# A pipelined decoder layer on one core: other mixtures, norm shifts on VectorE, low-rank halves, four product buffers, and another order

## The chip, the cores and the metric

The kernel runs on one core of a Trainium2 chip. The metric is the device time of one execution in microseconds (us). Everything is float32.

## The reference

The input `x` has 32 sequences of 256 tokens with 256 channels; `ctx` has the same shape. Three blocks are added to `x` in turn, each on a layer norm of it:

```python
# 1: RWKV layer
h  = layer_norm(n1, ln1_w, ln1_b); hh = h of the token before (0 for the first)
xk, xv, xr = h * tm + hh * (1 - tm)            # three mixtures with their own tm
k, v, sr = xk @ Wk.T, xv @ Wv.T, sigmoid(xr @ Wr.T)
y  = n1 + (sr * wkv(decay, first, k, v)) @ Wo.T     # a scan over the tokens
h  = layer_norm(y, ln2_w, ln2_b); xk, xr = two more mixtures
y  = y + sigmoid(xr @ Wrec.T) * (square(relu(xk @ Wkey.T)) @ Wval.T)
x  = x + y
# 2: attention of the 16 heads of one token among each other (16 values each)
x  = x + softmax(mask(q @ k.T / 4)) @ v       # q = norm(x), k = v = ctx, per token
# 3: low-rank feed-forward, rank 64
x  = x + (gelu((norm(x) @ U1) @ V1 + b1) @ U2) @ V2 + b2
```

## The kernel before

Two sequences, 512 tokens, make a group; there are NG = 16 groups. A group passes through five stages, and in step i of the program the engines work on group i-1 (here called A: mixtures, k, v, r, scan), i-2 (B: output projection, second norm, first key projections), i-3 (C: keys, values, third norm, attention scores) and i-4 (D: attention sums, fourth norm, low-rank block). `drive` lays the steps out: some unrolled ahead, a loop over pairs of steps, and some unrolled behind.

The program is written per engine. Each engine has a function `step` that lists its pieces in a fixed order with the semaphore waits between them; an engine works strictly in that order. TensorE (PE) does projections and transposes into eight PSUM banks of 512 columns; ScalarE (ACT) does activations; VectorE (DVE) does scans, residuals, statistics and sums of products; GpSimd (POOL) forms the products of the attention (`score_products`, `value_products`) and some sums and products of the scan; SyncE (SP) issues loads and stores.

- Norms: DVE takes statistics (`stats_of`, line 1154) and `mean_of` (1161). ACT forms ln of the variance and the negated mean (`variance_ln`, 440 and 441), rstd (`rstd_of`, 445), the shift -mean * rstd as four one-column activations (`shift_of`, 473), and `normalise` (480). For norm 1 there is also `back` (`scale_back`, 465), by which the normalised rows are scaled back.
- Mixtures: `now_part` (504, 506) writes the first token's column and then the present token's share from PSUM, `add_before` (1196) adds the share of the token before on DVE.
- Low-rank block: `project_u1` (904) writes the same 64 rows twice into one bank of 512 columns; `project_v1` (913) uses upper and lower half of the array in turn for even and odd output tiles; `project_u2` (920) sums even tiles in rows 0 to 63 and odd ones in rows 64 to 127; `project_v2` (932) multiplies with a doubled V2. `open_with_b2` (926) writes the bias. Each float32 matmul runs as two passes, each with its own weight load.
- Table loads: `use_table` (427) switches ACT between a set with exp and ln and one with tanh and gelu, four times per step.
- POOL works through D's scores 1 to 3 and values, and C's score block 0 at the end of its step; the products go through three buffers `prod`, so that a block waits for the sums of an earlier one.
- The norm chain ends in q (`normalise_3`), for which POOL's `score_products` (329) waits. `add_bb` on POOL forms the denominator, ACT's `ln_den` and `inverse_den` its reciprocal, and `divide_num` on POOL the numerator that `project_o` needs. `values_by_dim` (575) copies ctx.

## Time and profile before

| what | value |
|---|---|
| three runs, us | 1201.68, 1202.70, 1202.82; median 1202.7 |
| span of the profiled execution, us | 1199.4 |
| PE, DVE, ACT, POOL busy, us | 1020.8, 952.5, 940.2, 901.1 |
| PE weight loads busy, us | 586.0 |
| mean granted TensorE clock | 0.947 |

The profiled execution has no time of its own beside the span; the runs lie 1.8 to 3.4 us outside the span. Busy time is the time in which an engine executes at least one instruction. Pieces that follow each other directly overlap a little, so the mean time of an instruction times its count is more than the busy time.

### The profile page before, as it was taken

The page shows a single profiled execution, that of the slowest core. Times are in us where ns is not written, and L with a number is a line of the kernel's source. Part 1 is how long each engine was busy: PE and PEld are TensorE (multiplying, and loading weights), DVE is VectorE, ACT ScalarE, POOL GpSimd, SP SyncE. Part 2 cuts the span into 40 slices and gives each one's busy share as a digit, 9 for nine tenths or more (in the row PEclk, how much of TensorE's full clock was granted, in tenths as well). Part 3 has the DMA queues.
Part 4 walks back from the last instruction along what each step waited for, and adds up shares of the span by engine and source line. Part 5 has one row for each costly group of instructions (what it writes and reads, how often), then busy time and mean ns, then how long its engine had stood idle before and what let it go on. Part 6 is the DMA issues. An engine that isn't in the chain of part 4 may idle for free.

```text
span 1199.4 us, 14602 instructions
## 1 busy us (share of the span) xinstructions
PE 1020.8 (85%) x3584; PEld 586.0 (49%) x3584; DVE 952.5 (79%) x2092; ACT 940.2 (78%) x2007; POOL 901.1 (75%) x862
## 2 busy tenths in 40 slices
PE   2569698989899898989899898989898998969506
PEld 1237264654647363655646373645546473727202
DVE  3654889898989899798979898898979888757470
ACT  3778779888888979888888889888888888584504
POOL 0220997969696988969696978969696969978780
PEclk9889799999999999999999999999999999989767
DMA  5010020201111020201111110202011010201000
GB/s 176 18 23 31 1 53 1 71 0 54 18 54 19 9 62 1 72 0 53 18 53 18 33 38 1 72 0 62 9 53 36 17 37 0 54 1 36 1 17 18
DMA packets 38983, 38.54 MB, mean 32 GB/s; under 512 B 2932, under 2 KB 38648, under 8 KB 38904
## 3 DMA queue, kind: packets, MB, share of 16 engines
q1 hardware_dynamic: 30456, 29.38, 7.4%
q0 software_dynamic: 8448, 8.39, 4.6%
q14 instruction: 64, 0.52, 0.1%
q8 instruction: 15, 0.25, 0.1%
HBM read 29.38 MB, written 8.39 MB: 31 GB/s over the span
## 4 chain that ended last, share of the span: by engine, by line
PE 46%; ACT 25%; DVE 13%; issue 7%; POOL 6%; SPq 1%; DMA 0%; ACTq 0%; POOLq 0%; DVEq 0%
PE bank L832 18%; PE bank L889 12%; PE bank L920 5%; ACT n L480 4%; PE bank L839 4%; DVE bank L1345 4%; POOL prod L329 3%; ACT shift L473 3%; ACT q L480 3%; PE bank L913 3%; PE bank L932 2%; POOL prod L350 2%; DVE stat L1154 2%; ACT hidden L598 1%; ACT rr L546 1%
## 5 line engine op out<-in xcount | busy, mean ns | idle before, releaser
L329 POOL TENSOR_TENSOR prod<-q,kv_ctx 128x256 f32<-128x256 f32 (+5 forms) x448 | 360.1, 853 | 140.6 <-ACT q L480 140.6
L350 POOL TENSOR_TENSOR prod<-prob,v_dh 128x256 f32<-128x256 f32 (+3 forms) x256 | 383.9, 1606 | 0.0
L832 PE MATMUL bank<-xk,w_key 128*128 128x512 f32 x512 | 233.4, 605 | 11.3 <-DVE xk L1196 11.3
L889 PE MATMUL bank<-w_val,hidden 128*128 128x256 f32 x1024 | 225.9, 379 | 0.0
L1345 DVE TENSOR_REDUCE bank<-prod 128x64 f32<-128x256 f32 (+3 forms) x256 | 192.0, 819 | 34.8 <-POOL prod L350 25.4
L889 PEld LDWEIGHTS bank<-w_val,hidden 128*128 128x128 f32 x1024 | 193.5, 190 | 31.7 <-issue 6.7
L1318 DVE TENSOR_REDUCE score<-prod 128x16 f32<-128x256 f32 (+5 forms) x448 | 177.1, 466 | 19.5 <-POOL prod L329 19.4
L832 PEld LDWEIGHTS bank<-xk,w_key 128*128 128x128 f32 x512 | 97.7, 193 | 127.7 <-issue 111.0
L846 PE MATMUL bank<-ident,n 128*128 128x128 f32 x384 | 66.2, 302 | 103.4 <-ACT n L480 101.0
L565 ACT ACTIVATE hidden<-bank 128x512 f32<-128x512 f32 x128 | 74.1, 593 | 82.8 <-PE bank L832 82.7
L846 PEld LDWEIGHTS bank<-ident,n 128*128 128x128 f32 x384 | 49.3, 155 | 159.6 <-issue 153.7
L366 POOL TENSOR_TENSOR num<-num,rr 128x512 f32<-128x512 f32 x32 | 45.0, 1406 | 62.6 <-ACT rr L555 62.6
L427 ACT ACT_TABLE_LOAD x70 | 89.8, 1283 | 2.1 <-PEq L1494 0.9
L832 PE MATMUL bank<-xr,w_r 128*128 128x512 f32 x128 | 74.4, 711 | 16.9 <-DVE bb L1254 16.9
L598 ACT ACTIVATE hidden<-bank,vec 128x512 f32<-128x512 f32 x128 | 79.5, 710 | 6.3 <-PE bank L913 6.1
L832 PE MATMUL bank<-xk,w_k 128*128 128x512 f32 x128 | 64.4, 630 | 21.1 <-DVE xk L1196 21.1
L375 POOL TENSOR_TENSOR num<-num,aa 128x512 f32<-128x512 f32 x32 | 38.3, 1197 | 54.1 <-DVE num L1245 54.1
L1196 DVE SCALAR_TENSOR_TENSOR xk<-bank,prev_w,xk 128x510 f32<-128x510 f32 x64 | 47.1, 744 | 37.7 <-ACT xk L506 19.1
L569 ACT ACTIVATE hidden<-hidden 128x512 f32<-128x512 f32 x128 | 76.4, 627 | 0.0
L1364 DVE TENSOR_TENSOR y_out<-bank,x 128x512 f32<-128x512 f32 x32 | 22.0, 687 | 68.0 <-PE bank L932 67.9
L913 PE MATMUL bank<-pT,w_v 64*128 64x512 f32 x256 | 69.2, 640 | 6.4 <-ACT pT L594 6.3
L1154 DVE BATCH_NORM_STATS2 stat<-x 128x6 f32<-128x256 f32 x192 | 71.2, 413 | 1.7
(95 smaller groups left out, 1909.9 us busy)
## 6 DMA issues: line engine op xcount, KB each, us to landing
x_in<-in_x SPq DMA_DIRECT2D x16, 512.0 KB, 3.5
x<-in_x POOLq DMA_DIRECT2D x16, 512.0 KB, 5.7
kv_ctx<-in_ctx SPq DMA_DIRECT2D x16, 512.0 KB, 4.5
out<-y_out SPq DMA_DIRECT2D x16, 512.0 KB, 3.2
w_key<-in_wkey SPq DMA_DIRECT2D x1, 1024.0 KB
w_val<-in_wval SPq DMA_DIRECT2D x1, 1024.0 KB
w_k<-in_wk SPq DMA_DIRECT2D x1, 256.0 KB, 3.6
w_v<-in_wv SPq DMA_DIRECT2D x1, 256.0 KB, 4.4
```

What stands on the lines that cost most here:

```text
L329: ins = pool.tensor_tensor(o, a, b, ALU.mult)
L350: ins = pool.tensor_tensor(o, ph[:, HB * n:HB * n + HB, 0:keys].unsqueeze(2).to_broadcast(shape), vh[:, :, 0:keys].unsqueeze(1).to_broadca ...
L427: act.preload_act_table_set(name)
L480: ins = act.activation(dst[:, t, :], src[:, t, :], ACT.Identity, bias=shift[n][:, t:t + 1], scale=rstd[n][:, t:t + 1])
L598: act.activation(hidden[:, j, :], bank[HIDDEN_BANKS[j % 4]][:, :], ACT.Gelu_apprx_tanh, bias=vec[:, B1_AT + j:B1_AT + j + 1]).then_inc(gel ...
L832: mm = pe.matmul(to[:, :], w[:, fi, P * f:P * f + P], src[:, fi, :], start=(fi == 0), stop=(fi == CH - 1))
L846: mm = pe.transpose(to[:, P * t:P * t + P], src[:, t, P * f:P * f + P], ident[:, :])
L889: mm = pe.matmul(bank[6 + t // 2][:, C * (t % 2):C * (t % 2) + C], hidden[:, j, P * t:P * t + P], w_val[:, j, :], start=(j == 0), stop=(j ...
L913: pe.matmul(bank[HIDDEN_BANKS[j % 4]][:, :], w_v1[r:r + RANK, j // 2, :], pT[r:r + RANK, :], start=True, stop=True).then_inc(v1_mm, 1)
L1154: ins = dve.bn_stats(stat[n][:, t, :], src[:, t, :])
L1318: ins = dve.tensor_reduce(o, src, AX.X, ALU.add)
L1345: ins = dve.tensor_reduce(bank[5][:, row:row + HB * HD], src, AX.X, ALU.add)
```

## The change

- Mixtures: ACT writes the share of the token before (`share_before`) and copies the first tokens' columns of both halves at once (`lone`); DVE adds the present token's share (`add_now`).
- Norms: the negated mean is gone; rstd is written beside the mean and a -1, and DVE forms the shift by one `tensor_reduce` with mult (`shift_of`), and `back` in the same way from two exponentials of ACT (`back_ratio`).
- Low-rank block: the two halves of rows now stand for the two halves of the tokens. `project_u1`, `project_v1`, `project_u2` and `project_v2` run on 256 columns per half; gelu reads its 512 columns from two banks.
- Four `prod` buffers. `n4` shares memory with `n2`, and `y_out` is gone: the last residual is written into `x3`.
- Banks are given out anew, transposes and the two parts of `rec` have banks of their own, and `project_v2` of a group runs at the start of the next step.
- x is loaded two steps ahead, after the store in SP's queue; one U1 load is gone, the two V1 loads carry all of V1 each.
- Each engine's `step` has another order. In the new one, with E = group i-5 and N = group i:

```
PE:   b2+v2(E) key4(C) tr1_0(A) key5-7(C) rec0,1(C) tr1_1(A) val0,1(C) k0(A) val2,3(C) k1(A) o0,1(B) v0,1(A)
      tr4_0,1(D) u1(D) r0(A) v1_0,1(D) r1(A) v1_2(D) tr2_0(B) u2_0(D) tr2_1(B) v1_3(D) u2_1-3(D) key0-3(B)
ACT:  relu/square(C) with mixtures(A) and prob1(D) between, tanh rec(C), ln 1(N), denominators(B) with ctx copy(C),
      exponentials 0(A), norm 3(C), ceiling 0(A), ln 4, rstd 1, ratio, rstd 4, bonus 0(A), norm 4(D), exponentials 1(A)
      with n4T and pT copies and rstd 2, gelu 0-2(D), norm 2(B), gelu 3-5(D), shares k0 r0 r1(B), gelu 6,7(D),
      share k1(B), norm 1(N), tanh r(A), relu0(B), qT copy(D), prob0(C), relu1(B)
DVE:  mean 1(N) mass 1(D) last1(E) sum 1(D) mix r0(A) mass(D) mix k0(A) third0(D) mix k1 r1(A) sum 2(D) gate 0(C)
      mix v0(A) second0(C) stats 4(D) scan pp0(A) stats 3(C) sum 3(D) rise0(A) gate 1, second1, stats, mean 3(C)
      over_mass 1(D) SHIFT 3 third1, stats(D) mix v1(A) mean 4(D) scan pp1(A) SHIFT 4 rise1(A) first0,1, stats(B)
      SHIFT 1 weigh(A) mean 2(B) scan aa0(A) SHIFT 2 other scans(A) scores 0,1(C) top 0, mix k0 k1 r0 r1(B)
      gate_num0(A) scores 2 gate_num1(A) mass 0(C) scores 3 BACK top 1(C) stats 1(N+1) sum 0(C) last0(D)
POOL: score 1(D) add aa0(B) score 2,3(D) shift 0(D) add aa1(B) value 0(D) shift 1(D) value 1(D) add x(C)
      value 2,3(D) add bb0,1(B) divide 0,1(B) score 0(C)
```

The core of the diff:

```diff
+    LAST = NG + 5
+    LOOP = (6, 14)
...
+        TR1_BANK = [7, 1]
+        K_BANK = [3, 0]
+        V_BANK = [7, 1]
+        R_BANK = [4, 6]
+        O_BANK = [6, 4]
+        TR2_BANK = [7, 2]
+        REC_BANK = [3, 2]
+        KEY_BANK = [0, 2, 7, 3, 6, 4, 6, 1]
+        VAL_BANK = [0, 6]
+        TR4_BANK = [6, 2]
+        U1_BANK, DOWN_BANK = 6, 3
+        LOW_BANK = [6, 3, 1, 1]
+        HIGH_BANK = [7, 2, 0, 0]
+        Y_BANK = [0, 2]
...
-                act.activation(nmean[n][:, :], mv[n][:, :, 0], ACT.Copy, scale=-1.0).then_inc(nmean_done[n], 1)
...
-            def shift_of(n, g):
-                act.wait_ge(nmean_done[n], upto(g, 1))
-                act.wait_ge(rstd_done[n], upto(g, 1))
-                for t in range(TT):
-                    ins = act.activation(shift[n][:, t:t + 1], nmean[n][:, t:t + 1], ACT.Identity,
-                                         scale=rstd[n][:, t:t + 1])
-                ins.then_inc(shift_ready[n], 1)
...
+            def back_ratio(g, par):
...
+                act.activation(ratio[par][:, :, 0], lnc[:, :], ACT.Exp, scale=0.5)
+                act.activation(ratio[par][:, :, 1], lnv[1][:, :], ACT.Exp, scale=-0.5).then_inc(ratio_done, 1)
...
+            def share_before(dst, f, src, m):
+                if f == 0:
+                    act.activation(dst[:, :, :].rearrange("p c (s t) -> p c s t", s=SEQ)[:, :, :, 0],
+                                   lone[:, CH * m:CH * m + CH, :], ACT.Copy)
+                norm = MIXES[m][1]
+                return act.activation(seqs(dst, f)[:, :, 1:T], by_seq(src)[:, :, 0:T - 1], ACT.Identity,
+                                      bias=col(norm + "_b", f), scale=before_w[:, CH * m + f:CH * m + f + 1])
...
             def project_u1(g):
                 pe.wait_ge(n4T_done, upto(g, 2))
                 for fi in range(CH):
-                    mm = pe.matmul(bank[3][:, :], w_u1[:, fi, :], n4T[:, fi, :],
-                                   start=(fi == 0), stop=(fi == CH - 1))
+                    for e in range(2):
+                        mm = pe.matmul(bank[U1_BANK][RANK * e:RANK * e + RANK, 0:W // 2], w_u1[:, fi, :],
+                                       n4T[:, fi, W // 2 * e:W // 2 * e + W // 2],
+                                       start=(fi == 0), stop=(fi == CH - 1))
                 mm.then_inc(u1_mm, 1)
 
             def project_v1(g, jj):
-                if jj == 0:
-                    pe.wait_ge(pT_done, upto(g, 1))
+                pe.wait_ge(pT_done, upto(g, 1))
                 for j in (2 * jj, 2 * jj + 1):
-                    r = RANK * (j % 2)
-                    pe.matmul(bank[HIDDEN_BANKS[j % 4]][:, :], w_v1[r:r + RANK, j // 2, :],
-                              pT[r:r + RANK, :], start=True, stop=True).then_inc(v1_mm, 1)
+                    at = (W // 2) * (j % 2)
+                    for e, to in ((0, LOW_BANK[jj]), (1, HIGH_BANK[jj])):
+                        rows = slice(RANK * e, RANK * e + RANK)
+                        mm = pe.matmul(bank[to][:, at:at + W // 2], w_v1[rows, j, :], pT[rows, :],
+                                       start=True, stop=True)
+                mm.then_inc(v1_mm, 1)
 
             def project_u2(g, jj):
...
+                for t in range(2):
+                    for e in range(2):
+                        rows = slice(RANK * e, RANK * e + RANK)
+                        mm = pe.matmul(bank[Y_BANK[e]][:, C * t:C * t + C], qT[rows, P * t:P * t + P],
+                                       w_v2[rows, :], start=False, stop=(t == 1))
...
+            def shift_of(n, g):
+                dve.wait_ge(rstd_done[n], upto(g, 1))
+                dve.tensor_reduce(shift[n][:, :], mv[n][:, :, :], AX.X, ALU.mult).then_inc(shift_ready[n], 1)
...
+            def scale_back(g, par):
...
+                dve.tensor_reduce(back[par][:, :], ratio[par][:, :, :], AX.X, ALU.mult).then_inc(back_done, 1)
...
-            def add_before(dst, f, src, name):
-                m = MIXES.index(name)
-                x = src[:, :].rearrange("p (s t) -> p s t", s=SEQ)
-                out = seqs(dst, f)[:, :, 1:T]
-                return dve.scalar_tensor_tensor(out=out, in0=x[:, :, 0:T - 1], scalar=prev_w[:, m, f:f + 1],
-                                                in1=out, op0=ALU.mult, op1=ALU.add)
...
+            def add_now(dst, f, src, m):
+                return dve.scalar_tensor_tensor(out=dst[:, f, :], in0=bank[src], scalar=now_w[:, CH * m + f:CH * m + f + 1],
+                                                in1=dst[:, f, :], op0=ALU.mult, op1=ALU.add)
...
+                dve.wait_ge(n4_done, upto(g, 1))
                 if s == 0 and some(g):
                     dve.wait_ge(out_stored, 16 * g)
-                dve.wait_ge(v2_mm, upto(g, 2, s + 1))
-                dve.tensor_tensor(pair(y_out, s), bank[s][:, :], pair(x3[par], s), ALU.add).then_inc(y_done, 1)
+                dve.tensor_tensor(pair(x3[par], s), bank[Y_BANK[s]], pair(x3[par], s), ALU.add).then_inc(y_done, 1)
...
```

## Rows read from the trace of the kernel before

**Rows 1.** Windows of single steps: us, then busy time (x instructions) per engine, clock, DMA.

```profile
88.00:150.40 62.40, 51.86 (x165) 31.36 (x164) 38.15 (x89) 49.16 (x103) 30.26 (x36) 0.86 0.05 17
150.40:217.30 66.90, 61.17 (x217) 34.85 (x216) 57.66 (x129) 57.96 (x125) 56.85 (x54) 0.97 0.10 24
...
484.30:551.70 67.40, 63.29 (x226) 36.47 (x225) 59.01 (x131) 58.20 (x125) 56.15 (x54) 0.97 0.12 32
551.70:618.20 66.50, 62.80 (x226) 36.46 (x225) 59.18 (x131) 58.05 (x125) 56.26 (x54) 0.97 0.12 32
...
1019.00:1085.40 66.40, 56.54 (x207) 34.66 (x206) 45.51 (x105) 42.07 (x84) 56.06 (x53) 0.92 0.11 25
...
1150.00:1199.40 49.40, 18.43 (x56) 7.17 (x56) 16.14 (x31) 12.08 (x24) 15.02 (x10) 0.63 0.03 11
```

**Rows 2.** Chain of waits, 551 to 686 us: start us, us, what.

```profile
554.36 10.30 PE bank L832 x24
...
575.89 6.92 PE bank L889 x32
...
586.12 0.86 ACT shift L473 x4
...
587.07 2.08 ACT q L480 x4
...
605.30 1.29 ACT hidden L598 x2
...
609.72 1.01 PE bank L920 x4
610.72 1.92 PE bank L832 x4
612.64 1.87 PE bank L920 x8
...
615.56 1.06 PE bank L932 x4
...
618.34 0.86 PE bank L932 x4
```

**Rows 3.** Groups by line: out<-in, shapes, count, busy us, mean ns, idle before.

```profile
L473 ACT ACTIVATE shift<-nmean,rstd 128x1 f32<-128x1 f32 x256 | 54.0, 282 | 3.6 <-ACT rstd L445 0.4
...
L904 PE MATMUL bank<-n4T,w_u 128*128 128x512 f32 x64 | 36.5, 698 | 4.5 <-ACT n4T L588 4.3
...
L504 ACT ACTIVATE xr<-bank,first_b,now_w 128x2 f32<-128x2 f32 x64 | 23.9, 373 | 0.8 <-PE bank L846 0.8
...
L465 ACT ACTIVATE back<-lnc,half 128x1 f32<-128x1 f32 x64 | 13.5, 288 | 0.0
...
L441 ACT ACTIVATE nmean<-mv 128x4 f32<-128x4 f32 x64 | 12.1, 190 | 0.0
```

**Rows 4.** Groups by line, the two smallest kinds of DVE operation.

```profile
L1161 DVE BATCH_NORM_AGGREGATE mv<-stat 128x2 f32<-128x6 f32 x256 | 23.9, 155 | 1.0
...
L1334 DVE RECIPROCAL mass<-mass 128x32 f32<-128x32 f32 x32 | 11.0, 343 | 0.0
```

**Rows 5.** Timeline of PE weight loads, 603 to 617 us: start us, us, what.

```profile
608.26 0.19 PEld L913 LDWEIGHTS bank<-pT,w_v 64*128 64x128 f32 x2 [0.23 <-issue]
...
613.05 0.14 PEld L920 LDWEIGHTS bank<-hidden,w_u 128*64 128x64 f32 x2 [0.29 <-issue]
```

**Rows 6.** Groups by line, the two product helpers of POOL.

```profile
L350 POOL TENSOR_TENSOR prod<-prob,v_dh 128x256 f32<-128x256 f32 (+3 forms) x256 | 383.9, 1606 | 0.0
L329 POOL TENSOR_TENSOR prod<-q,kv_ctx 128x256 f32<-128x256 f32 (+5 forms) x448 | 360.1, 853 | 140.6 <-ACT q L480 140.6
```

**Rows 7.** Waits by engine: total us, times, longest.

```profile
POOL prod L329 <- ACT q L480: 140.6, 16, 11.3
```

**Rows 8.** Timeline of PE in the last group: start us, us, what.

```profile
1178.32 3.75 PE L904 MATMUL bank<-n4T,w_u 128*128 128x512 f32 x4 [0.89 <-ACT n4T L588]
...
1193.34 1.99 PE L932 MATMUL bank<-w_v,pT 128*128 128x256 f32 x8
```

More of the change, by code:

```diff
@@ L127, in build @@
         n2 = sb("n2", [P, TT, C])
+        n4 = n2
         gate_rec = sb("gate_rec", [P, TT, C])
@@ L134, in build @@
         v_dh = sb("v_dh", [P, TT, HD, NH])
-        prod = [sb(f"prod{s}", [P, max(S_SIZE, V_SIZE)]) for s in range(3)]
+        prod = [sb(f"prod{s}", [P, max(S_SIZE, V_SIZE)]) for s in range(4)]
         score = sb("score", [P, TT * NH, NH])
@@ L585, in copy_n4T @@
                 act.wait_ge(tr4_mm, upto(g, 2, f + 1))
-                if f == 0 and some(g):
+                if some(g):
                     act.wait_ge(u1_mm, upto(g - 1, 1))
-                act.activation(n4T[:, f, :], bank[4][:, :], ACT.Copy).then_inc(n4T_done, 1)
+                act.activation(n4T[:, f, :], bank[TR4_BANK[f]], ACT.Copy).then_inc(n4T_done, 1)
             def copy_pT(g):
@@ new lines, in step @@
+                if on(4):
+                    copy_pT(i - 4)
+                if on(1):
+                    use_table(EXP_SET)
+                    exp_bonus(i - 1, 1)
+                if on(1):
+                    use_table(EXP_SET)
+                    exp_e1(i - 1, 1)
+                if on(4):
+                    use_table(GELU_SET)
+                    if on(3):
+                        act.wait_ge(val_mm, upto(i - 3, 9, 2))
+                    elif on(5):
+                        act.wait_ge(down_mm, upto(i - 5, 4, 1))
+                    gelu(i - 4, 0)
@@ L1025, in step @@
                     elif on(5):
-                        pe.wait_ge(qT_done, upto(i - 5, 1))
-                    transpose_4(i - 4, 0)
+                        pe.wait_ge(y_done, upto(i - 5, 2))
+                    transpose_4(i - 4, 1)
+                if on(4):
+                    if on(4):
+                        pass
+                    elif on(2):
+                        pe.wait_ge(x1_done, upto(i - 2, 2, 1))
+                    elif on(3):
+                        pe.wait_ge(x2_done, upto(i - 3, 2))
+                    elif on(5):
+                        pe.wait_ge(gelu_done, upto(i - 5, 8, 2))
+                    project_u1(i - 4)
@@ new lines, in step @@
+                    project_v1(i - 4, 3)
+                    project_u2(i - 4, 1)
+                    project_u2(i - 4, 2)
+                    project_u2(i - 4, 3)
+                if on(2):
+                    if on(4):
+                        pe.wait_ge(gelu_done, upto(i - 4, 8))
+                    elif on(1):
+                        pe.wait_ge(bb_done, upto(i - 1, 2))
+                        pe.wait_ge(aa_done, upto(i - 1, 2))
+                    elif on(3):
+                        pe.wait_ge(x2_done, upto(i - 3, 2, 1))
+                    elif on(5):
+                        pe.wait_ge(y_done, upto(i - 5, 2, 1))
+                    project_key(i - 2, 0)
@@ L1169, in mean_1, with shift_1, shift_2, shift_3 @@
                 mean_of(1, g)
+            def shift_of(n, g):
+                dve.wait_ge(rstd_done[n], upto(g, 1))
+                dve.tensor_reduce(shift[n][:, :], mv[n][:, :, :], AX.X, ALU.mult).then_inc(shift_ready[n], 1)
+            def shift_1(g):
+                shift_of(1, g)
+            def shift_2(g):
+                shift_of(2, g)
+            def shift_3(g):
+                shift_of(3, g)
+            def shift_4(g):
+                shift_of(4, g)
+            def scale_back(g, par):
+                dve.wait_ge(ratio_done, upto(g, 1))
+                if some(g - 1):
+                    dve.wait_ge(x1_done, upto(g - 2, 2))
+                dve.tensor_reduce(back[par][:, :], ratio[par][:, :, :], AX.X, ALU.mult).then_inc(back_done, 1)
             def stats_2(g, par, s):
@@ L1295, in second_residual @@
                 dve.wait_ge(x_added, 16 * (g + 1))
-                dve.scalar_tensor_tensor(out=pair(x2[par], s), in0=bank[6 + s][:, :], scalar=0.5,
+                if some(g - 1):
+                    dve.wait_ge(x3_done, upto(g - 2, 2, s + 1))
+                dve.scalar_tensor_tensor(out=pair(x2[par], s), in0=bank[VAL_BANK[s]], scalar=0.5,
                                          in1=pair(x1[par], s), op0=ALU.mult, op1=ALU.add).then_inc(x2_done, 1)
@@ L1466, in step @@
                 if on(3):
-                    sum_mass(i - 3, 0)
-                    sum_mass(i - 3, 1)
+                    sum_values(i - 3, 0, 0)
+                    inverse_mass(i - 3, 0)
+                if on(4):
+                    last_residual(i - 4, p, 0)
             drive(dve, step, step, step)
```

1091 lines of the change are left out of this document (654 added, 437 removed).

## The prediction

> **What bounds the kernel now.** I read the page first. PE leads with 1020.8 of 1199.4 us, DVE has 952.5, ACT 940.2 and POOL 901.1: no engine is full, so the time lies in how they hand over. The windows of one step each show a steady state: from 150 to 1019 us there are 13 steps of 66.8 us, and in one of them PE is busy about 62.5, DVE 59.2, ACT 58.1 and POOL 56.2 us [rows 1]. The chain of waits says how a step closes. It has two stretches. In the first PE runs without a gap, from the first key projection (610.7 in one step) through the second output of low rank, the other keys (10.30 us) and the two value pieces of 6.9 us: by the same pieces one step earlier it ends at 582.8 [rows 2]. With the step of 66.8 that is 582.8 + 66.8 - 610.7 = 38.9 us. The second stretch, 582.8 to 610.7, 27.9 us, is a staircase: gate and norm statistics on DVE, then 21 us of ACT without a gap (norms 3, 4 and 2 with their shifts, the exponentials, mixtures, the first two gelus), then 4 us of PE. So a step is one stretch of PE and one of ACT in a row, 38.9 + 27.9.
>
> **The change, part by part.**
>
> *Low-rank halves.* `project_u1` was 4 passes of 512 columns on the whole array; it becomes 8 passes of 256 on two column halves. It costs 36.5 / 16 = 2.3 us per group [rows 3], 4 x 0.43 = 1.7 of it at the full clock. If the halves run together that is 4 x 0.216 = 0.9 us, where 0.216 is a 256-column pass in the value pieces (6.91 us for 32) [rows 2]. `project_v2` goes from 8 passes (1.06 + 0.86 us [rows 2]) to 4 pairs, 0.9 to 1.0 us. `project_v1` and `project_u2` have twice the passes at half the length, so the same columns. They run at half price already; what is new is that a pair has 0.216 us in which to load two pairs of weights. The rows show that two loads for two row halves end together in 0.19 us and two for column halves in 0.14 [rows 5]; both fit under 0.216. Bounds: nothing, or, were each load on its own as 0.19 per pass, 32 x 0.19 - 4.0 = +2.1 us per step for `project_v1`. I take nothing, as the rows are of the same operation. The copies of pT and qT halve: 0.25 us each.
>
> Here two rules speak against the change. The rows have weight loads of one column pair under the pair before it (0.14 us every 0.43) [rows 5]. The Trainium skill, "TensorE: Matmul & The Clock Gate", The mechanism, says that a load overlaps running matmuls only when its row group differs. By that rule the 20 column pairs of `project_u1` and `project_u2` would each show their 0.14 us, 12 more than now, +1.7 us per step and up to 22 us in all, 1170; this trace disagrees, and I give it no more than a part of the chance of the halves' rival below. And four passes of `project_u2` take 1.01 us on the chain between other shapes where two pairs at full rate need 0.86 [rows 2]. The Trainium skill, "TensorEngine Tiling (Array Packing)", Key Properties, says that changing the tiling mode drains TensorE; the trace agrees, at about 0.15 us.
>
> Counted in the code, the new order changes the shape of the array about 13 times per step, the old one 10; at those 0.15 us that is +0.4 us, inside the slack I add below.
>
> *Norm shifts.* ACT loses the four negated means (0.19 us each in the row, 0.10 on the path) and 16 one-column products, 54.0 / 64 = 0.85 us per norm [rows 3]; `back` (13.5 / 16 = 0.85 per step) and `half` become two small exponentials. DVE gains five reductions of 4 x 3 or 4 x 2 elements. The trace has no such reduction; the nearest rows are 155 ns (aggregate, 6 elements) and 343 ns (reciprocal, 32) [rows 4]. I take 0.17 each, the end with the like size: DVE +0.85 us per step, 1.7 at the upper bound. A hop from ACT to DVE and back adds two semaphores, 0.1 us, against 0.95 saved: 0.8 gained per norm if DVE is there. The reduction stands in DVE's queue behind whatever is in front of it, and what is behind it waits for ACT: this is the slower rival.
>
> *Mixtures.* The order of the two products is swapped, ACT writes the share of the token before (one PSUM input), DVE adds the present one. Both keep their sizes (510 and 512 columns), so nothing changes but the first columns: 10 one-column activations per group of 0.37 each (0.24 on the path) [rows 3] become 5 copies of four columns. ACT -1.5 to -2.7 us per step; I take 2.
>
> ACT in sum: 3.4 + 0.8 + 0.5 + 2 + 0.5 = 7 us less, from 58.1 to about 51. PE from about 60 us of bare passes (62.5 with drains and slow stretches) to 58. DVE from 59.2 to 60.1, now the fullest engine. POOL stays at 56.2.
>
> *Order, banks, buffers.* The banks are spread so that few matmuls wait for a gate, and `project_v2` moves to the start of the next step. I laid the new order out by hand from these durations, starting at `project_v2`.
>
> PE stretch: four keys 6.9, b2 and v2 1.95, four keys 6.9, transposes 0.9, rec 3.45, values 13.8, first k 1.7: 35.6 us instead of 38.9. What left is the last half of `project_u2` (1.87 us, now under ACT's gelus [rows 2]), half of v2, and small gaps. Its conditions: relu 1 and 2 of ACT before v2, second `gate_num` before key 4, and `last_residual` of the group before, on DVE, before rec 1. By my sum DVE is 0.6 us early for the last; the others have 1 us or more.
>
> Staircase: value end to norm 3's logarithm 2.8 us (the last exponential of the first half ends 0.15 after the statistics). From there to the second gelu the old row of ACT work is 21.1 (0.6 of logarithm and rstd before the shift at 586.12, to the end of two gelus at 606.6 [rows 2]); off it come three shifts 2.6 and their bits 0.5, the two gates of r 1.0, norm 2 (2.08) and a mixture pair (1.8), both moved later, and 0.3 of the pT copy; onto it come 0.6 (ceiling), 0.3 (ratio) and 0.3 of hops: 14.4. Then gelu 2, norm 2, gelus 3 to 5, three shares, gelus 6 and 7, the last k share, and one mixture on DVE: 6 x 0.64 + 2.1 + 3.1 + 0.7 = 9.8 [rows 2]. Sum 27.0: as long as now, since the key projections wait for all eight gelus.
>
> So 35.6 + 27.0 = 62.6 us with no slip. Two other loops come out as near. DVE's own work is 60.1 and two waits of 0.5 and 0.9 (second value, last k share): 61.5. And POOL: four score blocks of 5.63, four value blocks of 6.0 [rows 6], two adds, two shifts and a DMA issue are 52 us from q to the denominators, then ACT's logarithm, exponential, 2.0 us of `values_by_dim`, the second pair, the rise and its exponentials, and norm 3: 62.4. POOL waits for q 8.5 us per step now (140.6 us in 16 waits [rows 7]); the fourth buffer lets score 3 go without waiting for sums, and the wait shrinks to about 3.7. Three loops within 1.1 us of each other never all keep time, and I add 0.7: 63.3 us, 3.5 less per step.
>
> *Queues.* SP now holds a store behind the load of x that waits for norm 1, so a store starts some 46 us after its rows are ready. The residual that writes over that buffer comes 18 us after the store's 3 us in one case and 8 in the other (`last_residual` of the next group), and x lands 5 us before its statistics: nothing, and 1 to 2 us per step if norm 1 slips by 8. POOL's DMA issue stays where it was among the value blocks.
>
> *Ends.* First 150 us: the startup has one weight DMA less, nine more tiny DVE operations that lie under the load of x, shorter ACT pieces on two serial passes: -4 us. Last 180 us: the serial tails of the last groups have `project_u1` at 3.75 us, for half the columns 1.9, v2 at 1.99 for 1.0 [rows 8], shifts 0.8 twice, and a step of the common kind less 3: -7 us. The step that `project_v2` adds at the end holds nothing else.
>
> Sum: 13 x 3.5 = 45.5, + 4 + 7 = 56.5. Span 1199.4 - 56.5 = 1143; the runs' median 1202.7 is 3.3 us over the profiled span, so 1146. I say 1148.
>
> **Rivals.** *The loops bind harder than the sum.* DVE at 60.1 of 63 has no room, reductions cost 0.34, PE drains 0.4, and ACT, which is early now, waits for POOL's denominators. For it: in the old kernel PE has 60 of bare work and is still busy 62.5. Against it: ACT gains 7 us of room. Step 65.0: 13 x 1.8 = 23 and ends 7: 1172. *The gain is not there.* The layout has a wait I missed, such as rec 1 behind `last_residual` behind `sum_mass` behind the last relus, which puts 4 us back on PE's stretch: within 0.2% of 1202.7. *Slower: the shift reductions stop DVE.* DVE is in order; `shift_3`, `shift_4`, `shift_2` wait for ACT's rstd, and ACT may be in a 2.08 us normalise when the statistics arrive [rows 2]. If each of the three stops DVE for 2 us, DVE needs 60.1 + 6 + 1.4 = 67.5 and more with what it delays in turn, 69: 13 x 2.2 = +29, less 7 at the ends: 1225. It decides from 2.2 us of stop per shift on average. Against it: before each shift the order has 0.7 to 1.2 us of other DVE work, and ACT comes to each rstd about on time in my layout. *It does not do what it says:* the halves serialise, +2.1 on v1, +2 on u2 and none of the u1 gain, only part of it in the PE stretch: step 65.8, 1184.
>
> **How the numbers follow.** Forecast (62.6 to 64) 0.50; loops bind harder 0.24; even better than 62.6, as ACT's room is worth more than I see (1120) 0.05; halves serialise 0.06; gain not there 0.07 (0.04 of it within 0.2%); slower 0.08. A difference of 0.2%, 2.4 us, is about what a measurement of this kernel tells from no change. Faster 0.88, same 0.04, slower 0.08. The range leaves out the slow rival, the missing gain and the best end: 1128 to 1184. The floor is 60.1 of DVE per step, 13 x 6.7 and the ends, 1105.
>
> **What would show it.** In the profile after: step windows of 63 us with DVE at 60 and PE at 59 to 60; ACT near 51; `project_u1` under 1.1 us for 8 passes; `project_v1` 32 passes in about 4 us; DVE waiting for ACT at the shifts under 0.5 us each; POOL's wait for q at 3 to 5 us; chain shares with less PE. Wrong, if a step is over 65 or a shift's wait is among the longest.

## The result, and the profile after

| | before | after |
|---|---|---|
| median of 4 runs in one comparison, us | 1202.8 (1201.7 to 1204.2) | 1121.4 (1120.5 to 1122.4) |
| ratio, 95% interval | | 0.932 (0.931 to 0.934) |
| span of the profiled execution, us | 1199.4 | 1118.6 |
| PE, DVE, ACT, POOL busy, us | 1020.8, 952.5, 940.2, 901.1 | 981.2, 961.3, 831.6, 900.4 |
| mean granted TensorE clock | 0.947 | 0.957 |

The change took 81 us off, 27 more than forecast. The cheapest ruler is the start of `q` (norm 3), once per group. In the trace before it first stands at 120.5, then in 13 steps of 66.7 on average up to 987.8, then at 1052.0 and 1115.1. After it stands at 105.8, in 13 steps of 62.4 up to 917.4, then at 977.3 and 1036.9. So the 80.8 us of span are 14.7 ahead of the first `q`, 13 steps of 4.3 (55.7), 7.8 in the last two steps, and 2.6 behind the last `q`.

Windows of after from one `q` to the next (columns as in [rows 1]):

```profile
105.82:167.69 61.87, 49.35 (x167) 30.76 (x166) 56.71 (x125) 43.39 (x79) 56.03 (x53) 0.89 0.11 26
...
417.77:480.16 62.39, 60.10 (x261) 37.15 (x261) 59.62 (x136) 51.37 (x98) 56.08 (x53) 1.00 0.14 34
480.16:542.75 62.59, 60.43 (x262) 37.44 (x261) 59.60 (x136) 51.37 (x98) 56.09 (x53) 1.00 0.13 34
```

DVE and PE are busy 59.6 and 60.2 of 62.5 us, ACT 51.4. In every steady step the granted clock is 1.00. Groups of after that answer to [rows 3, 4, 8]:

```profile
L1429 DVE TENSOR_REDUCE shift<-mv 128x4 f32<-128x12 f32 x64 | 10.2, 159 | 5.7 <-ACT mv L456 3.5 <-ACT mv L468 1.3
L971 PE MATMUL psum<-n4T,w_u 128*64 128x256 f32 x128 | 19.1, 424 | 13.1 <-ACT n4T L597 13.1
L1004 PE MATMUL psum<-w_v,qT 64*128 64x256 f32 x128 | 18.1, 402 | 0.0
L502 ACT ACTIVATE xv<-lone 128x4 f32<-128x4 f32 x16 | 3.2, 199 | 1.3 <-PE psum L904 1.3
```

A shift is 0.16 us on DVE instead of 0.85 on ACT, u1 1.2 us per group instead of 2.3. The waits that answer to [rows 7], and the one by the shifts:

```profile
POOL prod L327 <- ACT q L480: 75.4, 16, 10.3
ACT q L480 <- DVE shift L1429: 4.6, 16, 0.3
```

A step's joint, in the timelines of three engines. PE from one start of the keys to the next; the last values end at 539.03:

```profile
502.87 7.11 PE L890 MATMUL psum<-xk,w_key 128*128 128x512 f32 x16 [0.27 <-DVE xk L1471]
509.91 1.13 PE L998 MATMUL psum<-b_row,ones 1*128 1x512 f32 x4
510.97 1.13 PE L1004 MATMUL psum<-w_v,qT 64*128 64x256 f32 x8
...
531.96 7.07 PE L944 MATMUL psum<-w_val,hidden 128*128 128x256 f32 x32
538.86 1.88 PE L890 MATMUL psum<-xk,w_k 128*128 128x512 f32 x4
...
544.84 3.67 PE L890 MATMUL psum<-xv,w_v 128*128 128x512 f32 x8 [0.39 <-DVE xv L1471]
548.73 1.06 PE L904 MATMUL psum<-ident,n 128*128 128x128 f32 x8 [0.22 <-ACT n L480]
550.64 1.08 PE L971 MATMUL psum<-n4T,w_u 128*64 128x256 f32 x8 [0.85 <-ACT n4T L597]
551.65 1.98 PE L890 MATMUL psum<-xr,w_r 128*128 128x512 f32 x4
...
556.15 1.98 PE L890 MATMUL psum<-xr,w_r 128*128 128x512 f32 x4 [0.58 <-ACT hidden L615]
...
562.38 2.81 PE L990 MATMUL psum<-hidden,w_u 128*64 128x256 f32 x24
565.46 2.81 PE L890 MATMUL psum<-xk,w_key 128*128 128x512 f32 x6 [0.27 <-DVE xk L1471]
```

DVE, from the second gate of values on, and where it gives the keys their input:

```profile
539.16 0.70 DVE L1575 SCALAR_TENSOR_TENSOR psum<-gate_rec,psum 128x512 f32<-128x512 f32 x1 [0.34 <-PE psum L944]
...
541.51 0.18 DVE L1417 BATCH_NORM_AGGREGATE mv<-stat 128x2 f32<-128x6 f32 x1
...
542.49 0.17 DVE L1429 TENSOR_REDUCE shift<-mv 128x4 f32<-128x12 f32 x1
...
563.87 1.44 DVE L1471 SCALAR_TENSOR_TENSOR xk<-psum,now_w,xk 128x512 f32<-128x512 f32 x2
```

ACT:

```profile
534.80 0.63 ACT L560 ACTIVATE rr<-rr 128x512 f32<-128x512 f32 x1 [4.63 <-POOL rr L370]
...
541.92 0.30 ACT L452 ACTIVATE lnv<-mv,eps_col 128x4 f32<-128x4 f32 x1 [0.59 <-DVE mv L1417]
...
542.75 2.08 ACT L480 ACTIVATE q<-x,shift,mv 128x256 f32<-128x256 f32 x4 [0.29 <-DVE shift L1429]
...
563.72 0.81 ACT L505 ACTIVATE xk<-psum,vec,before_w 128x510 f32<-128x510 f32 x1
```

From 541.9 to 564.5 ACT stops only 0.29 us. The view lists no stop of DVE from 539.2 to 565.2. PE, which starts the keys at 565.46, has no gap from 556.15 to 565.2. So the second half of a step is three runs side by side that end within about a microsecond of each other; my prediction saw ACT's alone.

Measured over ten steps of each trace, a step has three parts:

| us | keys start to end of values | end of values to `q` | `q` to the next keys |
|---|---|---|---|
| before | 38.7 to 39.3 | 4.3 to 4.4 | 23.5 to 23.8 |
| after | 36.15 | 3.5 or 3.7 | 22.7 to 22.8 |

So about 2.8 of the 4.3 us per step were gained in TensorE's stretch, and about 1.6 in the staircase behind it. The rows say what left the stretch: the last half of `u2`, 1.87 us [rows 2], which no longer stands behind the first key, and half of v2.

### The profile page after: what moved, and what is told of

Its sections match the earlier page's. It is cut to its first block and busy times, and to the rows that moved or that the text cites. A ratio compares the mean times of both kernels' runs of the same rounds, so it can differ in the third digit from the quotient of the medians.

```text
span 1118.6 us, 15640 instructions
## 1 busy us (share of the span) xinstructions
PE 981.2 (88%) x4160; PEld 608.8 (54%) x4160; DVE 961.3 (86%) x2185; ACT 831.6 (74%) x1557; POOL 900.4 (80%) x862
## 5 line engine op out<-in xcount | busy, mean ns | idle before, releaser
L890 PE MATMUL psum<-xk,w_key 128*128 128x512 f32 x512 | 233.9, 607 | 17.1 <-DVE xk L1471 17.1
L944 PE MATMUL psum<-w_val,hidden 128*128 128x256 f32 x1024 | 225.9, 379 | 0.0
L1634 DVE TENSOR_REDUCE psum<-prod 128x64 f32<-128x256 f32 (+3 forms) x256 | 191.9, 818 | 24.1 <-POOL prod L349 24.1
L944 PEld LDWEIGHTS psum<-w_val,hidden 128*128 128x128 f32 x1024 | 193.5, 190 | 31.7 <-issue 6.7
L890 PEld LDWEIGHTS psum<-xk,w_key 128*128 128x128 f32 x512 | 95.3, 193 | 132.3 <-issue 128.9
L574 ACT ACTIVATE hidden<-psum 128x512 f32<-128x512 f32 x128 | 75.9, 593 | 79.9 <-PE psum L890 79.6
L615 ACT ACTIVATE hidden<-psum,vec 128x512 f32<-128x512 f32 x128 | 80.8, 689 | 7.2 <-PE psum L982 6.1
L890 PE MATMUL psum<-xk,w_k 128*128 128x512 f32 x128 | 63.6, 624 | 15.8 <-DVE xk L1471 15.8
L1408 DVE BATCH_NORM_STATS2 stat<-x 128x6 f32<-128x256 f32 x192 | 71.6, 416 | 1.7
L982 PE MATMUL psum<-pT,w_v 64*128 64x256 f32 x512 | 70.9, 410 | 2.0 <-ACT pT L603 1.7
L890 PE MATMUL psum<-xr,w_r 128*128 128x512 f32 x128 | 62.5, 614 | 7.6 <-ACT hidden L615 7.6
L480 ACT ACTIVATE n<-x,shift,mv 128x256 f32<-128x256 f32 x128 | 66.1, 592 | 0.9 <-DVE shift L1429 0.9
```

The source lines that it names most:

```text
L574: act.activation(hidden[:, j, :], bank[KEY_BANK[j]], ACT.Relu).then_inc(relu_done, 1)
L615: act.activation(seqs(hidden, j), both_halves(j), ACT.Gelu_apprx_tanh, bias=vec[:, B1_AT + j:B1_AT + j + 1]).then_inc(gelu_done, 1)
L890: mm = pe.matmul(to[:, :], w[:, fi, P * f:P * f + P], src[:, fi, :], start=(fi == 0), stop=(fi == CH - 1))
L944: return pe.matmul(bank[VAL_BANK[t // 2]][:, C * (t % 2):C * (t % 2) + C], hidden[:, j, P * t:P * t + P], w_val[:, j, :], start=(j == 0), ...
L982: mm = pe.matmul(bank[to][:, at:at + W // 2], w_v1[rows, j, :], pT[rows, :], start=True, stop=True)
L1634: ins = dve.tensor_reduce(bank[SUM_BANK][:, row:row + HB * HD], src, AX.X, ALU.add)
```

## The experiments

All but the last start from the changed kernel (1121.4 us); each ran four times, beside the kernel before on the same chip, whose median was 1202.0 to 1203.0. Steps are the distances of `q`.

| kernel | us | ratio to before, 95% | first `q` | steady step |
|---|---|---|---|---|
| after | 1121.4 | 0.931 to 0.934 | 105.8 | 62.4 |
| f1_gates | 1134.5 | 0.941 to 0.946 | 118.8 | 62.5 |
| f2_residual | 1129.1 | 0.938 to 0.942 | 113.7 | 62.5 |
| f3_fill | 1134.7 | 0.943 to 0.946 | 119.7 | 62.5 |
| s3_three | 1121.7 | 0.932 to 0.935 | 107.2 | 62.5 |
| s1_shift_act | 1242.5 | 1.031 to 1.035 | 113.3 | 71.6 |
| s4_shift_only | 1183.4 | 0.984 to 0.988 | 109.1 | 65.8 to 67.6 |
| s2_full_rank | 1145.6 | 0.951 to 0.954 | 106.6 | 64.0 |
| m1_mixtures | 1135.2 | 0.942 to 0.946 | 109.5 | 63.2 |
| p1_idle | 1122.0 | 0.932 to 0.936 | 106.9 | 62.5 |
| p2_stair | 1146.0 | 0.951 to 0.956 | 105.6 | 63.4 or 65.0 |
| p3_dve | 1123.4 | 0.934 to 0.937 | 106.2 | 62.5 |
| p4_dve_run | 1136.2 | 0.944 to 0.948 | 106.6 | 63.6 |
| n1_order | 1135.4 | 0.941 to 0.945 | 106.4 | 63.3 |
| n2_ceiling | 1122.8 | 0.932 to 0.936 | 106.2 | 62.5 |
| n3_r_first | 1123.3 | 0.932 to 0.936 | 107.5 | 62.5 |
| b1_shift_old | 1212.8 | 1.008 to 1.012 | 124.3 | 67.6 (67.2 to 68.4) |

### The fill: f1, f2, f3

```diff
 # f1, steps -2 to 2 only
-ACT: ..., norm 2, ..., norm 1, gate r 0, gate r 1, relu 0, ...
+ACT: ..., gate r 0, norm 2, gate r 1, ..., relu 0, ..., norm 1
+PE: each r projection waits for bb_done and aa_done of its half
 # f2, steps -2 to 2 only
-DVE: residual 0, stats, residual 1, shift 1, stats, weigh 0, mean 2, scan aa 0, shift 2, ...
+DVE: residual 0, stats, shift 1, weigh 0, scan aa 0, residual 1, scan bb 0, stats, weigh 1, mean 2, scan aa 1, scan bb 1, shift 2, ...
-PE: o 0, o 1, v 0, v 1
+PE: o 0, v 0, o 1, v 1
 # f3: both
```

> The changed kernel with one thing put back, and only in the steps before the first q (steps -2 to 2 of the fill): the r projections wait for both scans as when r shared the banks of k, the r gates stand around norm 2 as before and norm 1 stands behind them. Theory 'order' (the 14.7 us that the fill got shorter come from what stands ahead of norm 1 and norm 2 on ScalarE and VectorE, not from shorter instructions): transposes of the second group at 43 to 46 us instead of 38.3, the first q 6 to 9 us later, the steps after it unchanged, so 1127 to 1131 us. Rival 'pieces' (the fill got shorter because the mixtures, shifts and halves are fewer or shorter pieces, which this kernel keeps): within 2 us of 1121.4.

> The changed kernel with the other half of the fill's order put back in steps -2 to 2: the second residual, its statistics and mean 2 between the scans on VectorE, and the second output projection behind the first of v on TensorE. Theory 'order': mean 2 of the first group 3 to 5 us later, and norm 2 and the first q with it: 1124 to 1127 us. Rival 'pieces': within 2 us of 1121.4.

> Both of the above together. Theory 'order': the first q comes 11 to 15 us later, near the 120.5 us of the kernel before, and the steps of 62.5 us stay: 1132 to 1136 us. Rival 'pieces': under 1125 us.

f1 moved the first `q` by 13.0 us, more than the 6 to 9 expected, f2 by 7.9 instead of 3 to 5, f3 by 13.9: 'order' holds, 'pieces' falls, and the two halves don't add, as both delay the same norm 2. The transposes of the second group start at 45.8 us in before, 38.4 in after and 44.4 in f3; norm 2 of the first group on ACT, in the same three:

```profile
73.18 2.07 ACT L480 ACTIVATE n<-x,shift,rstd 128x256 f32<-128x256 f32 x4
```

```profile
59.99 2.06 ACT L480 ACTIVATE n<-x,shift,mv 128x256 f32<-128x256 f32 x4
```

```profile
73.14 2.08 ACT L480 ACTIVATE n<-x,shift,mv 128x256 f32<-128x256 f32 x4 [0.66 <-DVE shift L1449]
```

In f3 norm 2 is back to within 0.04 us of before, with all the shorter pieces still in, and with x still loaded two steps ahead. The chain is: r in banks of its own need not wait for the scans over k's banks, so its gates don't hold up norm 1, whose group's mixtures stand on ACT ahead of the first group's denominator; and with both residuals ahead of the scans, mean 2 is there earlier. The pieces are not free in the new order, though: without the short shifts the first `q` comes 3.3 us later (s4), without the short mixtures 3.7 (m1). Order and pieces don't add up here.

### One part taken out: s3, s1, s4, s2, m1

```diff
 # s3_three
-prod = [... for s in range(4)]
+prod = [... for s in range(3)]      # slots and waits as before the change
```

> The changed kernel with three product buffers, in the slots and with the waits that the kernel before had. Theory 'circle' (a step is as long as TensorE's stretch plus ScalarE's run from mean 3 to the keys; the product buffers only feed GpSimd and VectorE beside it): GpSimd waits about 4.4 us per step for q anyhow, so a part of the new waits is absorbed there; I expect 0 to 2 us per step, 1121 to 1150 us. Rival 'the fourth buffer carries the gain': the steps go back by 3 us or more each, over 1165 us.

The steps did not change: the fourth buffer is worth nothing here (1121.7 us). POOL's wait for `q` stays at 75.9 us in all.

```diff
 # s1_shift_act                      (s4_shift_only: shifts alone, back stays on DVE)
+nmean = Copy(mv[n][:, :, 0], scale=-1.0)                  # ACT
-tensor_reduce(shift[n], mv[n], X, mult)                   # DVE
+for t in range(TT): shift[n][:, t] = Identity(nmean[n][:, t], scale=mv[n][:, t, 1])   # ACT
-tensor_reduce(back[par], ratio[par], X, mult)             # DVE
+for t in range(TT): back[par][:, t] = Exp(lnc[:, t], bias=half[:, t], scale=0.5)      # ACT
```

> The changed kernel, its order kept, with the shifts and the scale back made on ScalarE as before (a negated mean and four one-column pieces per norm, a halved logarithm and four one-column exponentials) and no reductions for them on VectorE. Theory 'circle' (a step is TensorE's stretch plus ScalarE's run from mean 3 to the keys, with nothing to spare): the shifts of norms 3, 4 and 2 and the scale back all lie in that run, 0.6 + 0.9 + 0.9 + 0.3 us less what VectorE's answer cost there, so 2.4 to 2.8 us per step and 1156 to 1164 us; VectorE's 0.6 us less per step give nothing. Rival 'VectorE binds': the step stays or falls, 1112 to 1122 us.

It came out 1242.5, slower than the kernel before. About 2.6 us per step of it are my own doing: the scale back writes a buffer that the residuals of two groups earlier read, and at this place in ACT's order it waits for them.

```profile
ACT back L482 <- DVE x L1587: 33.7, 14, 2.7
```

The steps run at a clock of 0.93, with TensorE idle for 5.5 us ahead of n4's transposes. How the rest divides between that clock and the pieces' own time I did not separate. s4 leaves the scale back out:

> The changed kernel with the four shifts alone made on ScalarE as before (a negated mean and four one-column products per norm); the scale back stays a reduction on VectorE, so that its wait for the residuals of s1_shift_act is gone. Theory 'circle': 0.6 us for norm 3, 0.9 each for norms 4 and 2: 2.4 us per step. The second theory, new with p2_stair, is that a gap of TensorE ahead of u1 that grows from 0.85 to over 1.8 us brings a stretch at the lower of its two clocks, 1.8 us more: then 4.2 us per step and a granted clock of 0.97 or less per step, 1170 to 1185 us; without it the clock stays at 1.00 and the time is 1153 to 1160 us. Rival 'VectorE binds': 1112 to 1124 us.

1183.4 us, in the range of the second theory, and 4.3 us more per step on average. PE in a late step of s4, and the clock of two steps in a row:

```profile
512.18 1.25 PE L920 MATMUL psum<-ident,n 128*128 128x128 f32 x8 [2.15 <-ACT n L492]
514.11 1.97 PE L987 MATMUL psum<-n4T,w_u 128*64 128x256 f32 x8 [0.69 <-ACT n4T L609]
516.01 3.78 PE L906 MATMUL psum<-xr,w_r 128*128 128x512 f32 x4
```

```profile
505.15:572.49 67.34, 62.97 (x262) 38.19 (x261) 59.45 (x133) 55.04 (x117) 56.36 (x53) 0.95 0.12 32
572.49:638.52 66.03, 61.51 (x262) 37.83 (x261) 59.38 (x133) 54.86 (x117) 56.27 (x53) 0.97 0.13 32
```

After idles of 2.15 and 0.69 us the next passes take 1.97 and 3.78 us where after has 1.08 and 1.98: the lower clock, half speed. But my split of the 4.2 us was wrong. The one steady step without a dip takes 65.8 us, 3.4 more than in after and not 2.4; those at 0.97 take 66.0 to 66.4, those at 0.95 67.3 to 67.6. So by this one step a dip costs 0.2 to 1.8 us here, and the shifts with what they push 3.4: 1.2 between the last values and `q`, 2.2 from `q` to the keys. Norm 4 starts 4.9 us after `q` instead of 3.8, and norm 2 11.1 after norm 4 instead of 10.0. Each shift costs about 1.1 us in this run, with its negated mean and the hand-over to the next piece, not the 0.6 to 0.9 that I took.

```diff
 # s2_full_rank
-u1, v1, u2, v2 on 256 columns in two halves of the array; pT, qT 256 columns; gelu from two banks
+u1, v1, u2 on 512 columns, v2 with all 128 rows; pT, qT 512 columns; gelu from one bank
```

> The changed kernel with the low-rank block as before the change: u1 for both halves of the rows at once over 512 columns, v1 and u2 over 512 columns, v2 with all 128 rows of qT, pT and qT copied over 512 columns; its place in the order is kept. Theory 'circle': u1 grows by 1.1 us in ScalarE's run (its copy waits for it) and that copy by 0.2, v2 by 1.0 us in TensorE's stretch, v1 and u2 stay, so 1.5 to 2.3 us per step and 1144 to 1156 us. Rival 'halves are free of effect' (two column tiles of half width cost what one full pass costs): within 3 us of 1121.4. Rival 'halves cost': faster than 1118 us.

1.5 us per step, 1145.6 us, in the range of 'circle': 0.7 in TensorE's stretch (v2) and 0.8 between `q` and the keys (u1). u1 takes 35.3 us in all instead of 19.1, u2 62.0 instead of 63.2: twice the passes and weight loads of half the length cost u2 1.2 us over 16 groups. The Trainium skill, "TensorE: Matmul & The Clock Gate", The mechanism, says that a load overlaps running matmuls only when its row group differs. By that each load of the halves would stand alone; this trace contradicts it.

```diff
 # m1_mixtures
-ACT: copy of the first columns; share of the token before (510);  DVE: + share now (512)
+ACT: first columns, one piece per half; share now (510);          DVE: + share of the token before (510)
```

> The changed kernel with the mixtures made as before: ScalarE writes the present token's share in two pieces (two first columns, then 510), VectorE adds the share of the token before. In ScalarE's run lie four of the first-column pieces, 0.24 us each, less the two copies of 0.10: 0.75 us per step, 1131 to 1134 us, if the clock stays at 1.00. Rival 'free': the mixtures' pieces are hidden, within 3 us of 1121.4. Rival 'the clock goes': gaps of TensorE grow past what it bears, granted clock 0.97 per step, 1150 us and over.

The step grew by 0.77 us, where 0.75 was expected, at a clock of 1.00, and the first `q` came 3.7 later: 1135.2 us. TensorE's wait ahead of the keys went from 0.27 to 0.70.

Together the parts taken out cost 13.3 + 0.3 + 62.0 + 24.2 + 13.8 = 114 us, against 81 for the whole change. They are prices in this order, not shares. None of them returns the whole of the 2.8 us that TensorE's stretch got shorter: s2 returns 0.7, and the rest, which the rows give to the place of `u2`, was not put back in a run.

### Work put in: p1, p2, p3, p4

```diff
 # p1_idle:    ACT ahead of ln_den 0: 20 copies 128x4;  POOL ahead of its wait for q: 20 memsets 128x4
 # p2_stair:   ACT ahead of the copies of n4T: 10 copies 128x4
 # p3_dve:     DVE ahead of sum_scores(3): 2 reductions 128x4 <- 128x512
 # p4_dve_run: DVE ahead of sum_scores(0): the same 2 reductions
```

> The changed kernel with work added where two engines wait anyway: twenty copies of 128x4 more per step on ScalarE (some 2.0 us) ahead of the logarithm of the denominator, where it stands idle 4.6 us, and twenty tiny memsets on GpSimd (2 to 4 us in all by its other fixed costs) ahead of its wait for q of 4.4 us. Theory 'circle': none of it is in the circle, 1120 to 1125 us. Rival 'ScalarE or GpSimd binds': 2 us and more per step, over 1150 us.

Nothing in the steps (1122.0 us); ACT's idle of 4.63 became 2.71, POOL's 4.40 became 3.78. Both additions stand ahead of a wait, so this shows that the two idles are idle, and not how much room POOL's whole loop has.

```profile
531.08 2.00 ACT L708 ACTIVATE spare<-eps_col 128x4 f32<-128x4 f32 x20
535.79 0.63 ACT L563 ACTIVATE rr<-rr 128x512 f32<-128x512 f32 x1 [2.71 <-POOL rr L371]
```

> The changed kernel with ten copies of 128x4 more per step on ScalarE, ahead of the copies of n4's transposes, some 0.10 us each, so in ScalarE's run. Theory 'circle': every step gets longer by what they take, 1.0 us, 1134 to 1138 us. Rivals 'VectorE binds' or 'GpSimd binds' (ScalarE is only 74% busy): within 3 us of 1121.4.

0.94 us in most steps, as expected, but 2.4 to 2.5 in four steady ones that ran at 0.97. The profiled execution took 1140.0 us at a mean clock of 0.952; the other three took 1146.0 to 1149.7 at 0.943 to 0.946. The median of 1146.0 is 8 over the upper end. TensorE's idle ahead of u1 is 1.8 us in both kinds of step (303.2 and 366.5):

```profile
303.18 1.08 PE L974 MATMUL psum<-n4T,w_u 128*64 128x256 f32 x8 [1.80 <-ACT n4T L598]
304.20 1.98 PE L893 MATMUL psum<-xr,w_r 128*128 128x512 f32 x4
...
366.51 1.90 PE L974 MATMUL psum<-n4T,w_u 128*64 128x256 f32 x8 [1.79 <-ACT n4T L598]
368.33 2.82 PE L893 MATMUL psum<-xr,w_r 128*128 128x512 f32 x4
```

> The changed kernel with two reductions over 512 elements more per step on VectorE (1.2 to 1.3 us) ahead of the last sum of scores, so in front of its idle moments of 0.8 and twice 0.3 us. Theory 'circle': VectorE is not in the circle at that place and swallows most of it, 0 to 0.3 us per step, 1121 to 1127 us. Rival 'VectorE binds' (it is the fullest engine beside TensorE, 59.6 of 62.5 us): 1.2 us per step, 1137 us and over.

0.04 us per step for 1.27 us of work; the 2 us in all arose mainly ahead of the second `q` and in the last two steps.

> The changed kernel with the same two reductions (1.27 us) as in p3_dve, but ahead of the first sum of scores, between the last bonus product and the mixtures of keys. New reading of the trace after: from the second gate of values (539.2) to the mixtures of keys (565.2) VectorE has no gap either, so the second half of the circle is VectorE's run and ScalarE's run at once, and only its place tells whether VectorE binds. That reading: 1.0 to 1.3 us per step, TensorE's gap ahead of the keys grows from 0.27 to some 1.4 us, 1136 to 1142 us, and 1150 or more if that gap brings TensorE's lower clock. Old theory 'ScalarE alone makes the second half': as p3_dve, within 3 us of 1123.4.

The same work 14 us earlier in DVE's queue costs 1.1 us per step, at a clock of 1.00:

```profile
424.09:487.62 63.53, 60.09 (x261) 37.19 (x261) 60.66 (x138) 51.34 (x97) 56.32 (x53) 1.00 0.14 33
```

So DVE's run is in the circle and its idle moments beyond it are not: 'ScalarE alone makes the second half' falls.

### Attempts to go further: n1, n2, n3

```diff
 # n1_order, ACT
-both_ln, ln_den 0, inverse 0, values_by_dim, ..., exp e2 0, ln 3, rstd 3, q, ceiling 0, ln 4, both_rstd, back_ratio, rstd 4, bonus 0, norm 4
+both_ln, both_rstd, back_ratio, values_by_dim, ln_den 0, inverse 0, ..., exp e2 0, ceiling 0, bonus 0, ln 3, rstd 3, q, ln 4, rstd 4, norm 4
 # n2_ceiling, ACT: only ceiling 0 moves, ahead of ln 3
 # n3_r_first: n2, and PE: r 0 ahead of u1; ACT: copy of pT behind bonus 1
```

> The changed kernel with another order on ScalarE: the exponentials for rstd 1 and the scale back right behind the two logarithms of norm 1, the copy of the values ahead of the logarithm of the denominator, and the ceiling and the bonus of the first half ahead of mean 3's logarithm. They leave ScalarE's run from mean 3 for the 4.6 us in which it waits for GpSimd. Theory 'circle': the run gets 0.3 + 0.6 + 0.6 us shorter, the step 1.0 to 1.5 us, until VectorE's 60.2 us of work per step decide: 1099 to 1108 us. Rival 'VectorE or GpSimd binds': within 3 us of 1121.4.

It lost 14 us. The move that I counted on freed nothing, as the first split waits for DVE's rise. The ceiling and the bonus then stand ahead of the logarithm of norm 3, which starts at 612.06 where mean 3 is ready at 611.05, and DVE's shift waits for it:

```profile
608.50 0.60 ACT L537 ACTIVATE psum<-rr 128x512 f32<-128x512 f32 x1 [1.12 <-DVE rr L1515]
...
612.06 0.28 ACT L452 ACTIVATE lnv<-mv,eps_col 128x4 f32<-128x4 f32 x1
...
612.61 0.17 DVE L1429 TENSOR_REDUCE shift<-mv 128x4 f32<-128x12 f32 x1 [0.97 <-ACT mv L456]
...
616.42 2.08 ACT L480 ACTIVATE n<-x,shift,mv 128x256 f32<-128x256 f32 x4 [0.73 <-DVE shift L1429]
```

So `q` comes 4.5 to 4.7 us after the last values instead of 3.5 or 3.7, and that is the whole loss. From `q` to the keys it takes 22.6 us, as long as in after (22.7): what left that place gave back no more than DVE's answers, now uncovered (0.73 us ahead of norm 4), took.

> The changed kernel with one instruction moved on ScalarE: the ceiling of the first half (0.6 us) ahead of the logarithm of norm 3, where ScalarE stands idle 0.59 us. n1_order moved five and lost 0.8 us per step, because two of them pushed that logarithm back by 0.8. Theory 'circle': ScalarE's run gets up to 0.6 us shorter, part of it lost to TensorE's transposes of norm 4, 0.2 to 0.6 us per step, 1112 to 1119 us. Rival 'VectorE's shift decides norm 4' (it stands behind a scan and comes at 546.2 where the norm starts at 546.5): 0 to 0.2 us per step, 1118 to 1122 us.

> n2_ceiling with one more move: TensorE makes the first r projection ahead of u1, in the 0.85 us in which it waits for the copies of n4's transposes, and ScalarE copies pT behind the second bonus. Theory 'three runs end together' (ScalarE's, VectorE's and TensorE's own from the second gelu to the keys, within 0.3 us): no gain, 1119 to 1124 us. Rival 'TensorE's gap ahead of u1 counts': 0.5 us and more per step, 1110 to 1116 us.

Both kept the step at 62.5 us (1122.8 and 1123.3). In n2 ACT's idle of 0.59 is filled and norm 4 starts 0.2 us earlier after `q`, but the keys start 22.66 us after `q` instead of 22.71, waiting for DVE. Relief of 0.6 us on one run alone moved nothing; nothing I ran beats the changed kernel.

### One part in the old order: b1

```diff
 # b1_shift_old, from the kernel before
-ACT: negated means, four one-column products per norm
+DVE: mv with a third column of -1; tensor_reduce with mult behind mean 3, mean 4, mean 2 and for norm 1
-DVE: over_mass 1, gate_values 1, ..., mean 3
+DVE: gate_values 1, ..., mean 3, over_mass 1, shifts 3 and 1
```

> The kernel before, its order kept, with one part of the change: the four shifts are reductions with mult on VectorE, no negated means and no one-column products on ScalarE (the scale back stays there). The third place of mv holds -1, and the first of the two moves on VectorE is the sum's scaling of rows 16 to 31 behind mean 3 instead of ahead of the gate, to stand ahead of the shift. Taking the shifts back out of the changed kernel cost 62 us (s4_shift_only). Theory 'the price hangs on the order': here the part is worth the 2.4 us of ScalarE per step at most, as other waits stand behind it, 1168 to 1195 us. Rival 'the part is worth what taking it out costs': 1135 to 1150 us. Rival 'shifts stop VectorE' (my slower rival): over 1203 us.

1212.8 us, 0.8 to 1.2% slower than before, with ACT 3.3 us per step less busy. ACT in a step of b1:

```profile
594.42 2.08 ACT L469 ACTIVATE q<-x,shift,mv 128x256 f32<-128x256 f32 x4 [0.29 <-DVE shift L1161]
...
599.37 0.30 ACT L438 ACTIVATE lnv<-mv,eps_col 128x4 f32<-128x4 f32 x1 [0.57 <-DVE mv L1156]
...
605.95 0.30 ACT L438 ACTIVATE lnv<-mv,eps_col 128x4 f32<-128x4 f32 x1 [1.35 <-DVE mv L1156]
```

From the last values to `q` it takes 3.6 us instead of 4.3, so the shift of norm 3 does gain there. Behind `q` ACT's savings turn into waits for DVE's means; the keys start 24.9 to 25.5 us after `q` where before has 23.5 to 23.8. DVE sets that half here (from 590.9 to 613.4 it stops once, for 0.44 us), and it was given the work. From 190 to 1000 us DVE has no listed wait at a shift (12.5 us in seven waits outside, in the fill and at the end), so in the steps it is their work and places, with the moved scaling, and not the mechanism of my slower rival; which of these weighs most I did not separate.

## Why the prediction was off, step by step

- *Direction and parts: right.* u1 under 1.1 us for 8 passes (1.08 read), v1 in 4.3, the reductions 0.16 us where 0.17 was taken, ACT at 51.4 ("near 51"), DVE 59.6 (60), PE 60.2 (59 to 60), POOL's wait for `q` 4.4 us (3 to 5), ACT's wait for a shift 0.3 at most.
- *Layout: right in sum.* "35.6 + 27.0 = 62.6 us with no slip": 62.4 to 62.6 measured, as 36.15 of TensorE's stretch and 26.2 to 26.5 behind it. The second term was added up wrongly: the pieces listed for "14.4" give 14.0, so my own layout was 26.6 there and 62.2 in all, and TensorE's stretch was taken 0.55 too short.
- *Failed: "Three loops within 1.1 us of each other never all keep time, and I add 0.7".* They do keep time: after the fill all steps lie between 62.39 and 62.64. With 4.28 instead of 3.5 per step the 13 steps gave 55.7 us, not 45.5: 10.2 of the miss, of which the added 0.7 is 9.1. Nor were the three that near: 1.27 us put into DVE's loop cost 0.04 (p3), so the waits in my "61.5" shrink when it has more to do. That three runs end together makes the kernel touchy to edits (p2, p4, n1), not slow by itself.
- *Failed, and as large: "First 150 us ... -4 us".* It was -14.7. I priced the fill by shorter pieces and left out the order, though I had it by engine: f3 returns 13.9 us with every shorter piece in place, so that in the old order those pieces, with all else that stayed, are worth 0.8 us and not 4.
- *Mis-sized: the end.* 7.8 + 2.6 = 10.4 instead of 7. Behind the 14th `q`, s2 returns 5.2 us and s4 6.6, where my sum had 2.9 for the halves and 1.6 for the shifts. They don't add up to 10.4, and how it divides stays open.
- *Right by luck: what the second half is.* I called it ACT's. It is DVE's and ACT's at once (p2, p4), with PE's from the second gelu close by in the trace. Taking 0.6 us off ACT alone is worth nothing in this order (n2), and handing ACT's shifts to DVE in the old one costs about 1% (b1). The change cut ACT and at the same time moved DVE's second residual ahead of the scans and parted r from k's banks.
- *Doubts that fell.* The halves' loads are hidden (s2). The fourth buffer, to which I gave POOL's shorter wait, does nothing (s3). POOL's loop of "62.4" has slack: ACT stood idle for 0.59 us between it and the logarithm of norm 3, and n2 filled that at no cost. Where its end lies I did not find.
- *Met by luck: the rival "even better than 62.6 (1120) 0.05".* Its number came, its reason did not: the step is 62.4, and room on ACT is worth nothing by itself. The rest came from the fill and the end. In two other rivals I took 7 us for the ends where my sum has 11.
- *The slower rival* did not come: DVE stopped seven times in the whole execution for ACT at a shift, 0.9 us at the longest, 4.8 in all. f2 shows it in small: there shift 2 stands behind a scan that waits for ACT's exponential, and norm 2 starts at 67.5 instead of 60.0.

The difference of 24.3 us between the span that I summed (1143) and 1118.6 is 10.7 in the fill, 10.2 in the steps and 3.4 at the end. The 1148 held another 2 us that no term gives.

## What to carry to other kernels

Lay out the fill by the new order as carefully as a steady step: write down what stands ahead of the first group's critical pieces on each engine, since a gate or a shared bank there costs once what no shorter piece returns. For a steady step ask of every engine whether it has a gap in the stretch that decides, not how busy it is over the step; where two had none, an edit that relieved one was worth nothing (n2), and work added to either cost nearly in full (0.94 of 1.0 us in p2's steps without a dip, 1.1 of 1.27 in p4). The price of a part, found by taking it out of a finely fitted order, is not its worth in another order (62 us here, -11 in the old one).
